# The gathered rows of eight experts: turned into columns by transposing transfers of 16-bit halves instead of by TensorE

## The chip, the core and the metric

The kernel runs on one core of a Trainium2 chip. The metric is the device time of one execution in microseconds (us); three executions of the kernel before took 1567.37, 1568.19 and 1569.07 us, so the median is 1568.19 us. TensorE (PE) does matrix products and transposes, VectorE (DVE) and ScalarE (ACT) work elementwise, GpSimd (POOL) and SyncE (SP) here mostly start transfers (DMAs).

## The reference

A graph layer is followed by a feed-forward stack with a mixture of experts, on 625 tokens of 1024 numbers. Everything is float32.

```
x = x + gnn(layernorm(x), edges)                 # 625 x 1024, 10000 edges
h = layernorm(x) @ lin0_w + lin0_b
h = silu(h @ swi1_w1 + b1) * (h @ swi1_w2 + b2)
scores = softmax(h @ gate_w.T); topv, topi = top_k(scores, 4), renormalised
routed = sum over the 4 chosen experts e: topv_e * ((silu(h @ exp_w1[e]) * (h @ exp_w3[e])) @ exp_w2[e])
shared = (silu(h @ sh_w1) * (h @ sh_w3)) @ sh_w2  # hidden width 2048
h = (routed + shared) @ lin1_w + lin1_b
x = x + silu(h @ swi2_w1 + b1) * (h @ swi2_w2 + b2)
```

## The kernel before

**Arithmetic.** Activations lie with features on the 128 partitions and tokens along the free dimension. A float32 product is made of three faster products: each operand is cut into a high part (a copy in a shorter format) and a low part (the rest), and `hi*hi + hi*lo + lo*hi` is summed in PSUM (`products`, L1793). A weight matrix comes in units of 128 x 1024 numbers (128 output features, 8 input chunks). One unit is one SP transfer of 512 KB into one of four slots of `raw`; ACT writes the high part `w_hi` (L502) and DVE the low part `w_lo` (L1226), also in rings of four; PE then runs 8 chunks x 3 = 24 matmuls. A split waits until PE is done with the unit that was four places earlier, and SP reloads a slot of `raw` when both splits of the unit in it are done (`load_four`, L445).

**The stages.** Graph layer; `lin0` and `swi1`; the first half of the shared expert (`sha`: 16 units up, 8 down, 625 tokens each); the eight experts, fullest first, with 344, 332, 328, 324, 316, 312, 304 and 296 token slots; the second half of the shared expert; `lin1` and `swi2`. While `swi1` runs, its output is also turned to token-major rows (`h_rows`: PE transposes, ACT copies to `rows`, L876 and L878) and written to `h_rows_dram` by one ACT transfer (L907). Routing runs beside the first units of `sha` and leaves for each expert a list of token numbers.

**Into an expert.** POOL gathers the rows of an expert's tokens from `h_rows_dram` into `grow` (a view of `gath`), in three indirect transfers of 128, 128 and 88 rows (`gather`, L573). Features must lie on partitions, so PE transposes each 128-feature chunk `m` in three pieces into a PSUM bank (`expert_in`, L2151); ACT copies that to the high part `e_hi` (L916) and DVE computes the low part `e_lo` (L1569). For the first expert this follows unit `m` of the down projection of `sha`, for the others unit `m` of the down projection of the expert before.

**Through an expert.** Sixteen units up alternate between gate and value: ACT applies silu (L933), DVE multiplies (L1589), ACT and DVE split the product (L936, L1593). Eight units down follow. After each, ACT copies the result out of PSUM (`yt_copied`, L942), and PE turns the copy of the chunk before to rows (`turn_y`, L2172), which DVE copies to `yrow` (L1580, L1581) and POOL stores (L588). In instruction order PE runs down unit `m`, `turn_y(m - 1)`, `expert_in(next, m)`; after `m = 7` comes `turn_y(7)`. ACT runs in group `m`: split of the unit three ahead, copy out (L942), high part of the next expert's chunk (L916). DVE: split of the unit three ahead, `y_rows(m - 1)`, low part of the next expert's chunk.

Of the kernel before, what the change touches and what calls it, by code (L numbers as in the profile page):

```python
# [5 lines left out]
T = 625  # L6
D = 1024
EDGES = 10000
EXPERTS = 8
TOP = 4  # L10
P = 128
KC = D // P
# [12 lines left out]
SLOT_TILES = [(0, P), (P, P), (2 * P, CAP - 2 * P)]  # L25
RING = 4
# [21 lines left out]
def build(nc, x, src, dst, gnn_b, biases, gate, stream, out):  # L48
# [5 lines left out]
    u32 = mybir.dt.uint32  # L54
    ALU = mybir.AluOpType
# [3 lines left out]
    h_rows_dram = nc.dram_tensor("h_rows_dram", (T, D), f32).ap()  # L59
# [5 lines left out]
    with ctx:  # L65
# [16 lines left out]
        silu = sb("silu", [P, TP], f32)  # L82
        prod = sb("prod", [P, 2, TP], f32)
# [37 lines left out]

        acc = ctx.enter_context(nc.psum_tensor("acc", [P, 8, 512], f32))
# [9 lines left out]
        g_hi, g_lo = hl(act_b, KC, CAP)  # L132
# [9 lines left out]
        logits_t = gath[0:GW, D:D + TP]  # L142
        stats = silu[:, 0:NT * 12].rearrange("p (i h s) -> p i h s", i=NT, h=2)
# [209 lines left out]
        xe_tp = sem("xe_tp")  # L353
# [29 lines left out]
        ov_raw = grow[:, 1, :]  # L383
        ov_out = yrow[:, 0, :]
# [46 lines left out]
        def _(sp):  # L431
# [9 lines left out]

            def load_four(done, first):
                for s in range(RING):
                    sp.wait_ge(hi_split, done + (s + 1 - RING))
                    sp.wait_ge(lo_split, done + (s + 1 - RING))  # L445
                    sp.dma_start(raw[:, s, :],
                                 stream[bass.ds(first + s, 1), :, :].rearrange("u p n -> (u p) n")
                                 ).then_inc(raw_loaded[s], 16)
# [22 lines left out]
            with sp.Fori(U_SHA // RING + 1, U_EXP // RING) as g:  # L471
                load_four(g * RING, g * RING)
            sp.wait_ge(order_ready, 1)
            with sp.Fori(0, EXPERTS) as r:
                expert = sp.value_load(order_i[0:1, bass.ds(r, 1)], min_val=0, max_val=EXPERTS - 1)
                with sp.Fori(0, UNITS_EXPERT // RING) as g:
                    load_four(r * UNITS_EXPERT + g * RING + U_EXP, expert * UNITS_EXPERT + g * RING + U_EXP)
# [40 lines left out]
        def _(pool):  # L518
# [48 lines left out]
            def gather(e):  # L567
                pool.tensor_copy(now_tok[:, :], slot_tok[:, bass.ds(3 * e, 3)]).then_inc(now_ready, 1)
                pool.wait_ge(h_saved, 16)
                pool.wait_ge(now_ready, e + 1)  # L570
                pool.sem_inc(gather_go, 1)
                for n, (c0, cn) in enumerate(SLOT_TILES):
                    pool.indirect_dma_start(out=grow[0:cn, n, :], out_offset=None, in_=h_rows_dram,  # L573
                                            in_offset=bass.IndirectOffsetOnAxis(ap=now_tok[0:cn, n:n + 1], axis=0)
                                            ).then_inc(gathered, 16)
# [3 lines left out]
            pool.wait_ge(ln_tp, 2 * NT)  # L579
            gather(0)  # L580
# [10 lines left out]

            pool.wait_ge(xe_tp, KC)
            gather(1)
# [7 lines left out]
            with pool.If(fullest(pool) > CAP):  # L601
                pool.wait_ge(y_saved, 16 * 3 * EXPERTS)
                pool.wait_ge(xe_tp, EXPERTS * KC)
                pool.iota(ov_iota, [[1, OV_ALL]], base=CAP, channel_multiplier=0,
                          allow_small_or_imprecise_dtypes=True).then_inc(ov_ready, 1)
                with pool.Fori(0, OV_ROUNDS) as c:
                    with pool.Fori(0, EXPERTS) as e:
# [3 lines left out]
                        pool.indirect_dma_start(out=ov_in, out_offset=None, in_=h_rows_dram,  # L611
# [20 lines left out]
            pool.wait_ge(xe_tp, EXPERTS * KC)  # L632
# [12 lines left out]
        def _(act):  # L645
# [1720 lines left out]
```

## Time and profile before

| | |
|---|---|
| median of three executions | 1568.19 us |
| profiled execution: its own time | 1567.0 us |
| profiled execution: its span | 1565.3 us |
| share of the span busy: PE, DVE, ACT, POOL | 99%, 55%, 37%, 8% |
| mean traffic of the transfers | 131 GB/s |
| granted clock of TensorE | 0.999 of full speed |

The span runs from the first to the last instruction that the profiler recorded; the execution's own time is 1.7 us more. Matmuls are pipelined: the profile shows one of 312 columns as 309 ns long, although the next one starts about 0.15 us after it. The place of PE in time is therefore read from the chain of waits, which gives each group the time until the next one starts.

### The profile page before, as it was taken

What the parts mean: (1) busy time and instruction counts of PE and PEld (TensorE: products, weight loads), DVE (VectorE), ACT (ScalarE), POOL (GpSimd) and SP (SyncE); (2) the same over time, 40 slices, a digit from 0 to 9 for tenths busy, and PEclk for the clock granted to TensorE, in tenths of its full rate; (3) what the DMA queues carried; (4) which work ended last, traced back from release to release, by engine and by line L of the source; (5) the groups of instructions that cost most, each with busy time, mean ns of one, the idle gap of its engine ahead of it and who ended that gap; (6) DMA issues with size and microseconds to landing.
All of it is one profiled execution on the core that took longest, in us unless ns stands there. A gap on an engine that the chain in (4) does not pass through costs nothing.

```text
span 1565.3 us, 28095 instructions
## 1 busy us (share of the span) xinstructions
PE 1551.4 (99%) x10796; PEld 1534.7 (98%) x10796; DVE 854.2 (55%) x1460; ACT 584.7 (37%) x914; POOL 117.8 (8%) x139
## 2 busy tenths in 40 slices
PE   9999999999999999999999999999999999999998
PEld 9998999999999999999999999999999999999998
DVE  8665569845522344454544545454555366335886
ACT  6332345432222333343444444444444222223442
POOL 1321010000100001000010100001000133001000
PEclk9999999999999999999999999999999999999999
DMA  4412203232422446446464654646555576221333
GB/s 136 133 41 72 76 28 108 82 131 84 123 76 79 157 138 189 151 135 208 137 207 148 191 165 150 202 151 208 161 172 163 160 204 178 83 80 55 94 117 83
DMA packets 71001, 205.64 MB, mean 131 GB/s; under 512 B 13620, under 2 KB 22370, under 8 KB 70890
## 3 DMA queue, kind: packets, MB, share of 16 engines
q1 hardware_dynamic: 45020, 157.94, 32.6%
q0 software_dynamic: 14976, 32.81, 7.0%
q10 hardware_dynamic: 10894, 13.26, 2.7%
q8 instruction: 87, 1.43, 0.4%
q14 instruction: 24, 0.20, 0.0%
HBM read 185.01 MB, written 18.95 MB: 130 GB/s over the span
## 4 chain that ended last, share of the span: by engine, by line
PE 94%; DVE 4%; issue 1%; ACT 1%; ACTq 0%; DVEq 0%; POOL 0%; POOLq 0%
PE acc L1793 86%; PE acc L1773 2%; PE acc L2172 1%; PE acc L2151 1%; DVE w_lo L1277 1%; DVE yrow L1042 0%; PE acc L1842 0%; DVE yrow L1041 0%; ACTq L1000 0%; PE acc L2108 0%; PE acc L1758 0%; PE acc L2225 0%; PE acc L1784 0%; PE acc L1952 0%; DVE acc L1323 0%
## 5 line engine op out<-in xcount | busy, mean ns | idle before, releaser
L1793 PE MATMUL acc<-act_x,w_hi 128*128 128x312 f32 (+8 forms) x2304 | 507.6, 309 | 1.6 <-DVE act_b L1290 0.6
L1793 PE MATMUL acc<-act_b,w_hi 128*128 128x312 f32 (+8 forms) x2048 | 456.0, 311 | 0.0
L1793 PE MATMUL acc<-act_a,w_hi 128*128 128x314 f32 (+1 forms) x1920 | 423.0, 310 | 2.7 <-DVE gath L1349 2.3
L1793 PEld LDWEIGHTS acc<-act_x,w_hi 128*128 128x128 f32 x2304 | 385.3, 188 | 2.5 <-ACT act_a L826 1.0
L1793 PE MATMUL acc<-act_x,w_lo 128*128 128x312 f32 (+8 forms) x1152 | 355.7, 309 | 0.0
L1793 PEld LDWEIGHTS acc<-act_b,w_hi 128*128 128x128 f32 x2048 | 340.2, 189 | 0.1
L1226 DVE TENSOR_TENSOR w_lo<-raw,w_hi 128x1024 fp32r<-128x1024 f32 x253 | 309.0, 1222 | 44.2 <-ACT w_hi L502 43.2
L1793 PEld LDWEIGHTS acc<-act_a,w_hi 128*128 128x128 f32 x1920 | 319.5, 190 | 4.0 <-ACT w_hi L798 2.8
L1793 PE MATMUL acc<-act_b,w_lo 128*128 128x314 f32 (+8 forms) x1024 | 315.6, 308 | 0.0
L1793 PE MATMUL acc<-act_a,w_lo 128*128 128x314 f32 (+1 forms) x960 | 294.9, 307 | 0.0
L502 ACT ACTIVATE w_hi<-raw 128x1024 fp32r<-128x1024 f32 x264 | 277.1, 1051 | 8.3 <-PE acc L1793 4.6
L1793 PEld LDWEIGHTS acc<-act_x,w_lo 128*128 128x128 f32 x1152 | 216.7, 188 | 0.0
L1793 PEld LDWEIGHTS acc<-act_b,w_lo 128*128 128x128 f32 x1024 | 193.0, 188 | 0.0
L1793 PEld LDWEIGHTS acc<-act_a,w_lo 128*128 128x128 f32 x960 | 181.3, 189 | 0.0
L1589 DVE TENSOR_TENSOR prod<-acc,silu 128x344 f32<-128x344 f32 x64 | 33.1, 517 | 249.7 <-PE acc L1793 220.8
L936 ACT ACTIVATE act_b<-prod 128x344 fp32r<-128x344 f32 x64 | 31.5, 493 | 172.1 <-DVE prod L1589 172.1
L942 ACT ACTIVATE prod<-acc 128x344 f32<-128x344 f32 x64 | 29.3, 458 | 133.3 <-PE acc L1793 133.3
L1580 DVE COPY yrow<-acc 128x256 f32<-128x256 f32 x64 | 27.1, 423 | 75.3 <-PE acc L2172 75.3
L933 ACT ACTIVATE silu<-acc 128x344 f32<-128x344 f32 x64 | 29.4, 459 | 102.2 <-PE acc L1793 102.2
L1236 DVE TENSOR_TENSOR prod<-acc,silu 128x628 f32<-128x628 f32 x16 | 13.0, 811 | 99.3 <-PE acc L1793 99.3
L588 POOL DMA_DIRECT2D y_dram<-yrow x24 | 13.5, 563 | 681.1 <-DVE yrow L1581 680.7
L1569 DVE TENSOR_TENSOR act_x<-acc,act_x 128x344 fp32r<-128x344 f32 x64 | 33.1, 517 | 54.5 <-ACT act_x L916 53.9
(239 smaller groups left out, 1247.0 us busy)
## 6 DMA issues: line engine op xcount, KB each, us to landing
raw<-stream_dram SPq DMA_DIRECT2D x296, 512.0 KB, 3.7
y_dram<-yrow POOLq DMA_DIRECT2D x16, 512.0 KB
y_dram<-yrow POOLq DMA_DIRECT2D x8, 352.0 KB
rows<-x_dram ACTq DMA_DIRECT2D x1, 2500.0 KB
x_dram<-rows ACTq DMA_DIRECT2D x5, 500.0 KB
h_rows_dram<-rows ACTq DMA_DIRECT2D x1, 2500.0 KB
rows<-x_dram ACTq DMA_DIRECT2D x8, 312.5 KB
rows<-x_dram SPq DMA_DIRECT2D x5, 448.0 KB
```

The source lines that it names most:

```text
L502: nc.scalar.activation(w_hi[:, s, :], raw[:, s, :], ACT.Copy).then_inc(hi_split, count)
L933: act.activation(silu[:, 0:CAP], acc[:, 2 * m % 4, 0:CAP], ACT.Silu).then_inc(exp.silu, 1)
L936: act.activation(g_hi[:, m, :], prod[:, m % 2, 0:CAP], ACT.Copy).then_inc(exp.hi, 1)
L942: act.activation(prod[:, m % 2, 0:CAP], acc[:, m % 4, 0:CAP], ACT.Copy).then_inc(yt_copied, 1)
L1226: dve.tensor_tensor(w_lo[:, s, :], raw[:, s, :], w_hi[:, s, :].bitcast(f32), ALU.subtract).then_inc(lo_split, count)
L1277: dve.tensor_tensor(wlo8[:, n % 8, :], quad_source(q, t), whi8[:, n % 8, :].bitcast(f32), ALU.subtract).then_inc(dve_quad_lo, 1)
L1569: dve.tensor_tensor(e_lo[:, m, :], acc[:, TPB + 2 + m % 2, 0:CAP], e_hi[:, m, :].bitcast(f32), ALU.subtract).then_inc(xe_lo, 1)
L1580: dve.tensor_copy(yrow[:, 0:2, m * P:(m + 1) * P], b[:, 0:2 * P].rearrange("p (s d) -> p s d", d=P))
L1589: dve.tensor_tensor(prod[:, m % 2, 0:CAP], acc[:, (2 * m + 1) % 4, 0:CAP], silu[:, 0:CAP], ALU.mult).then_inc(exp.prod, 1)
L1773: last = pe.matmul(outs[i], oh_dst[0:TT, s, i * TT:i * TT + rows_of(i)], oh_src[0:TT, s, :], start=False, stop=ends)
L1793: ins = pe.matmul(o, w, xs_[h], start=(first and w is hi and xs_ is x_hi), stop=(last and w is lo))
L2151: last = pe.transpose(acc[:, TPB + 2 + m % 2, c0:c0 + cn], grow[0:cn, n, m * P:(m + 1) * P], ident[0:cn, 0:cn])
```

## The change

The gathered rows go from rows to columns in transfers rather than on PE. Such a transposing transfer handles 16-bit elements, so a float32 row is stored as two planes of 16-bit halves.

- `h_rows`: ACT reads the PSUM bank as 16-bit numbers and writes all first halves of a token's row and then all second halves (`rows16`, `h_rows_dram` of 2048 16-bit numbers per token).
- POOL gathers the same bytes, but for every expert after the first into one staging row per partition, `x_stage`, one third of the list at a time; each next third waits until the staging row has been turned. The first expert's three thirds go to `rows`.
- SP issues `dma_start_transpose` three times for each expert (128, 128 and 96 rows by 2048 halves), into `xe_parts`. For the first expert they follow the loads of the 16 up units of `sha`; for expert `e + 1` they follow the loads of units 11, 15 and 19 of expert `e`. SP's loops over the experts are written out.
- DVE puts the two halves of each number side by side again: one copy of 2 x 344 16-bit numbers for each chunk, into one of two buffers `x32`. ACT and DVE take high and low parts from there and no longer from PSUM.
- `expert_in` leaves PE's program. ACT takes the high part of the next expert's chunk `m` before its copy of unit `m`; DVE makes word `m` and low part `m - 1` before `y_rows(m - 1)`, and low part 7 before `y_rows(7)`.
- `silu` and `prod` become views of one tensor `work`, in which the experts have narrower views beside `x32`. A path for experts with more tokens than slots, which does not run on these inputs, is adapted as well.

```diff
+XR = 352
+YC = 3 * P
+X_TILES = [(0, P), (P, P), (2 * P, XR - 2 * P)]
+X_TURNS = (11, 15, 19)
...
-        silu = sb("silu", [P, TP], f32)
-        prod = sb("prod", [P, 2, TP], f32)
+        work = sb("work", [P, 3 * TP], f32)
...
+        silu = work[:, 0:TP]
+        prod = work[:, TP:3 * TP].rearrange("p (s w) -> p s w", w=TP)
+        e_silu = work[:, 0:CAP]
+        x32 = work[:, CAP:3 * CAP].rearrange("p (s w) -> p s w", w=CAP)
+        e_prod = work[:, 3 * CAP:3 * CAP + 2 * YC].rearrange("p (s w) -> p s w", w=YC)
...
+        x_stage = flat_b[:, 9 * D:10 * D].bitcast(u16)
...
+        xe_parts = gath[:, 0:KC * XR].bitcast(u16).rearrange("p (n s) -> p n s", s=XR)
+        xe_halves = xe_parts.rearrange("p (t k) s -> p t k s", t=2)
+        rows16 = rows[:, :, :].rearrange("p i d -> p (i d)").bitcast(u16).rearrange("p (i t d) -> p i t d", i=NT, t=2)
...
+            def turn_inputs(e, n, source, count):
+                c0, cn = X_TILES[n]
+                sp.wait_ge(gathered, 16 * count)
+                if e >= 1 and n == 0:
+                    sp.wait_ge(x32_ready, e * KC)
+                sp.dma_start_transpose(xe_parts[:, :, c0:c0 + cn], source[0:cn, :]).then_inc(xe_turned, 16)
+
+            with sp.Fori(U_SHA // RING + 1, (U_SHA + UNITS_UP) // RING) as g:
+                load_four(g * RING, g * RING)
+            for n in range(3):
+                turn_inputs(0, n, rows16[:, n, :, :].rearrange("p t d -> p (t d)"), 3)
+            with sp.Fori((U_SHA + UNITS_UP) // RING, U_EXP // RING) as g:
...
+            for r in range(EXPERTS):
+                expert = sp.value_load(order_i[0:1, r:r + 1], min_val=0, max_val=EXPERTS - 1)
+                for j in range(UNITS_EXPERT):
+                    load_one(r * UNITS_EXPERT + U_EXP + j, j % RING, expert * UNITS_EXPERT + U_EXP + j)
+                    if j in X_TURNS and r + 1 < EXPERTS:
+                        n = X_TURNS.index(j)
+                        turn_inputs(r + 1, n, x_stage, 3 * (r + 1) + n + 1)
...
+            def gather_tile(to, n):
+                cn = X_TILES[n][1]
+                pool.indirect_dma_start(out=to[0:cn, :], out_offset=None, in_=h_rows_dram,
+                                        in_offset=bass.IndirectOffsetOnAxis(ap=now_tok[0:cn, n:n + 1], axis=0)
+                                        ).then_inc(gathered, 16)
+
+            def gather_rest(e):
+                for n in range(1, 3):
+                    pool.wait_ge(xe_turned, e * (16 * 3) + 16 * n)
+                    pool.sem_inc(gather_go, 1)
+                    gather_tile(x_stage, n)
...
+            pool.wait_ge(x32_ready, KC)
+            pool.wait_ge(unit_done, U_EXP)
+            gather_list(1)
+            gather_tile(x_stage, 0)
+            gather_rest(1)
             with pool.Fori(1, EXPERTS - 1) as e:
+                pool.wait_ge(x32_ready, e * KC + KC)
+                gather_list(e + 1)
+                gather_tile(x_stage, 0)
                 save_y(e - 1)
-                pool.wait_ge(xe_tp, e * KC + KC)
-                gather(e + 1)
+                gather_rest(e + 1)
...
-                act.activation(rows[0:TT, 0:4, m * P:(m + 1) * P],
-                               acc[0:TT, TPB, :].rearrange("p (i d) -> p i d", d=P), ACT.Copy)
-                act.activation(rows[0:TT, 4, m * P:(m + 1) * P], acc[0:TT, TPB + 1, 0:P],
+                act.activation(rows16[0:TT, 0:4, :, m * P:(m + 1) * P],
+                               acc[0:TT, TPB, :].bitcast(u16).rearrange("p (i d t) -> p i t d", d=P, t=2), ACT.Copy)
+                act.activation(rows16[0:TT, 4, :, m * P:(m + 1) * P],
+                               acc[0:TT, TPB + 1, 0:P].bitcast(u16).rearrange("p (d t) -> p t d", t=2),
                                ACT.Copy).then_inc(h_copied, 1)
...
-                act.wait_ge(xe_tp, e * KC + (m + 1))
-                act.activation(e_hi[:, m, :], acc[:, TPB + 2 + m % 2, 0:CAP], ACT.Copy).then_inc(xe_hi, 1)
+                act.wait_ge(x32_ready, e * KC + (m + 1))
+                act.activation(e_hi[:, m, :], x32[:, m % 2, :], ACT.Copy).then_inc(xe_hi, 1)
...
+                    if nxt:
+                        expert_in_hi(e + 1, m)
                     act.wait_ge(unit_done, base + (UNITS_UP + m + 1))
                     if m >= 2:
                         act.wait_ge(y_tp, e * KC + (m - 1))
-                    act.activation(prod[:, m % 2, 0:CAP], acc[:, m % 4, 0:CAP], ACT.Copy).then_inc(yt_copied, 1)
-                    if nxt:
-                        expert_in_hi(e + 1, m)
+                    act.activation(e_prod[:, m % 2, 0:CAP], acc[:, m % 4, 0:CAP], ACT.Copy).then_inc(yt_copied, 1)
...
+            def expert_in_word(e, m):
+                if m == 0:
+                    dve.wait_ge(xe_turned, e * (16 * 3) + 16 * 3)
+                if m >= 2:
+                    dve.wait_ge(xe_lo, e * KC + (m - 1))
+                dve.tensor_copy(x32[:, m % 2, :].bitcast(u16).rearrange("p (s t) -> p t s", t=2),
+                                xe_halves[:, :, m, 0:CAP]).then_inc(x32_ready, 1)
+
             def expert_in_lo(e, m):
                 dve.wait_ge(xe_hi, e * KC + (m + 1))
-                dve.tensor_tensor(e_lo[:, m, :], acc[:, TPB + 2 + m % 2, 0:CAP], e_hi[:, m, :].bitcast(f32),
+                dve.tensor_tensor(e_lo[:, m, :], x32[:, m % 2, :], e_hi[:, m, :].bitcast(f32),
                                   ALU.subtract).then_inc(xe_lo, 1)
+
+            def expert_in(e, m):
+                expert_in_word(e, m)
+                if m >= 1:
+                    expert_in_lo(e, m - 1)
...
+                    if nxt:
+                        if m == 0:
+                            dve.wait_ge(unit_done, base + UNITS_UP)
+                        expert_in(e + 1, m)
                     if m >= 1:
                         y_rows(e, m - 1)
-                    if nxt:
-                        expert_in_lo(e + 1, m)
+                if nxt:
+                    expert_in_lo(e + 1, KC - 1)
                 y_rows(e, KC - 1)
...
-            def expert_in(e, m):
-                if isinstance(e, int):
-                    if m == 0:
-                        pe.wait_ge(gathered, 16 * 3 * (e + 1))
-                else:
-                    if m == 0:
-                        pe.wait_ge(gathered, e * (16 * 3) + 16 * 3)
-                if m >= 2:
-                    pe.wait_ge(xe_lo, e * KC + (m - 1))
-                for n, (c0, cn) in enumerate(SLOT_TILES):
-                    last = pe.transpose(acc[:, TPB + 2 + m % 2, c0:c0 + cn], grow[0:cn, n, m * P:(m + 1) * P],
-                                        ident[0:cn, 0:cn])
-                last.then_inc(xe_tp, 1)
...
+                    if e == 0 and j in (0, 2):
+                        pe.wait_ge(sha_y, KC - 1 + j // 2)
...
                         turn_y(e, m - 1)
-                    if nxt:
-                        expert_in(e + 1, m)
...
-            pe.wait_ge(sha_y, KC)
```

## Rows read from the trace of the kernel before

**Rows 1.** The page: span, busy time by engine, chain that ended last.

```profile
span 1565.3 us, 28095 instructions
PE 1551.4 (99%) x10796; PEld 1534.7 (98%) x10796; DVE 854.2 (55%) x1460; ACT 584.7 (37%) x914; POOL 117.8 (8%) x139
PE 94%; DVE 4%; issue 1%; ACT 1%; ACTq 0%; DVEq 0%; POOL 0%; POOLq 0%
```

**Rows 2.** Chain of waits in order of time: start us, us until the next, what.

```profile
509.97 0.70 ACT rows L923
...
575.64 3.82 PE acc L1793 x24
...
606.09 0.33 PE acc L2172 x3
606.42 0.30 PE acc L2151 x3
606.72 0.47 PE acc L2172 x3
...
1121.17 3.38 PE acc L1793 x24
1124.55 0.33 PE acc L2172 x3
```

**Rows 3.** Line L2151 alone: op, count, ns min/median/max, first and last start, forms.

```profile
L2151 PE MATMUL acc<-ident,gath x192: 240/272/273, 458.7 to 1144.9; 128*128 128x128 f32 x128, 88*128 88x88 f32 x64
```

**Rows 4.** Timeline of ACT: start us, us, line, op, out<-in, [idle before].

```profile
606.13 0.46 ACT L942 ACTIVATE prod<-acc 128x344 f32<-128x344 f32 x1 [2.41 <-PE acc L1793]
...
666.32 0.49 ACT L936 ACTIVATE act_b<-prod 128x344 fp32r<-128x344 f32 x1 [2.89 <-DVE prod L1589]
666.72 1.05 ACT L502 ACTIVATE w_hi<-raw 128x1024 fp32r<-128x1024 f32 x1
669.33 0.46 ACT L942 ACTIVATE prod<-acc 128x344 f32<-128x344 f32 x1 [1.57 <-PE acc L1793]
```

**Rows 5.** Timeline of DVE, same columns.

```profile
667.80 1.23 DVE L1226 TENSOR_TENSOR w_lo<-raw,w_hi 128x1024 fp32r<-128x1024 f32 x1
```

**Rows 6.** Groups of instructions by form on DVE: count, busy us, mean ns.

```profile
L1226 DVE TENSOR_TENSOR w_lo<-raw,w_hi 128x1024 fp32r<-128x1024 f32 x253 | 309.0, 1222 | 44.2 <-ACT w_hi L502 43.2
L1569 DVE TENSOR_TENSOR act_x<-acc,act_x 128x344 fp32r<-128x344 f32 x64 | 33.1, 517 | 54.5 <-ACT act_x L916 53.9
L1617 DVE TENSOR_SCALAR yrow<-gath,top_w 125x1024 f32<-125x1024 f32 x5 | 3.7, 745 | 0.0
```

**Rows 7.** Transfers by issue: count, size, us from issue to landing.

```profile
raw<-stream_dram SPq DMA_DIRECT2D x296, 512.0 KB, 3.7
gnn_bias<-gnn_b_dram SPq DMA_DIRECT2D x1, 4.0 KB, 10.9
```

**Rows 8.** Timeline of DVE in the seventh expert.

```profile
1066.99 1.22 DVE L1226 TENSOR_TENSOR w_lo<-raw,w_hi 128x1024 fp32r<-128x1024 f32 x1
...
1075.30 1.23 DVE L1226 TENSOR_TENSOR w_lo<-raw,w_hi 128x1024 fp32r<-128x1024 f32 x1
1080.01 0.52 DVE L1589 TENSOR_TENSOR prod<-acc,silu 128x344 f32<-128x344 f32 x1 [3.48 <-PE acc L1793]
1080.44 1.22 DVE L1226 TENSOR_TENSOR w_lo<-raw,w_hi 128x1024 fp32r<-128x1024 f32 x1
```

**Rows 9.** Timeline of ACT in the seventh expert.

```profile
1076.55 0.46 ACT L933 ACTIVATE silu<-acc 128x344 f32<-128x344 f32 x1 [1.28 <-PE acc L1793]
1078.41 1.06 ACT L502 ACTIVATE w_hi<-raw 128x1024 fp32r<-128x1024 f32 x1 [1.40 <-DMA raw<-stream_dram]
```

**Rows 10.** Timeline of ACT around `h_rows`, near the end of `swi1`.

```profile
315.14 0.58 ACT L876 ACTIVATE rows<-acc 125x512 f32<-125x512 f32 x1
...
316.63 0.94 ACT L831 ACTIVATE gath<-acc,bias 128x314 f32<-128x314 f32 x2 [0.74 <-DVE acc L1398]
```

**Rows 11.** Busy time by stretch, fourth to sixth expert: window, us; PE, PEld, DVE, ACT, POOL; clock, DMA share, GB/s.

```profile
791.70:1059.20 267.50, 267.50 (x1873) 266.93 (x1873) 134.30 (x193) 113.28 (x168) 14.53 (x21) 1.00 0.55 173
```

More of the change, by code:

```diff
@@ L131, in build @@
         e_hi, e_lo = hl(act_x, KC, CAP)
-        g_hi, g_lo = hl(act_b, KC, CAP)
+        flat_b = act_b[:, :, :].rearrange("p s n -> p (s n)")
+        g_hi, g_lo = [flat_b[:, s * KC * CAP:(s + 1) * KC * CAP].rearrange("p (k w) -> p k w", w=CAP)
+                      for s in range(2)]
+        x_stage = flat_b[:, 9 * D:10 * D].bitcast(u16)
         h_hi, h_lo = hl(act_b, NT, D)
@@ L383, in build @@
         ov_raw = grow[:, 1, :]
+        ov_x = grow[:, 2, :]
+        ov_words = sem("ov_words")
         ov_out = yrow[:, 0, :]
@@ L440, in _, with load_one @@
             sp.dma_start(bias[:, :, :], biases).then_inc(small_loaded, 16)
+            def load_one(done, s, u):
+                sp.wait_ge(hi_split, done + (1 - RING))
+                sp.wait_ge(lo_split, done + (1 - RING))
+                sp.dma_start(raw[:, s, :], stream[bass.ds(u, 1), :, :].rearrange("u p n -> (u p) n")
+                             ).then_inc(raw_loaded[s], 16)
             def load_four(done, first):
                 for s in range(RING):
[L444 to L448, printed above, removed]
+                    load_one(done + s, s, first + s)
             def load_seven(L):
@@ L571, in gather @@
                 pool.sem_inc(gather_go, 1)
-                for n, (c0, cn) in enumerate(SLOT_TILES):
-                    pool.indirect_dma_start(out=grow[0:cn, n, :], out_offset=None, in_=h_rows_dram,
-                                            in_offset=bass.IndirectOffsetOnAxis(ap=now_tok[0:cn, n:n + 1], axis=0)
-                                            ).then_inc(gathered, 16)
+            def gather_tile(to, n):
[8 more added lines that the diff above has]
+                    gather_tile(x_stage, n)
             pool.wait_ge(routed, 1)
             pool.wait_ge(tok_copied, 1)
-            pool.wait_ge(ln_tp, 2 * NT)
-            gather(0)
+            gather_list(0)
+            for n in range(3):
+                gather_tile(rows16[:, n, :, :].rearrange("p t d -> p (t d)"), n)
             pool.wait_ge(tok_copied, 4)
@@ L610, in _ @@
                         pool.sem_inc(ov_go, 1)
-                        pool.indirect_dma_start(out=ov_in, out_offset=None, in_=h_rows_dram,
+                        pool.indirect_dma_start(out=ov_in.bitcast(u16), out_offset=None, in_=h_rows_dram,
                                                 in_offset=bass.IndirectOffsetOnAxis(ap=now_tok[:, 0:1], axis=0)
@@ L906, in _ @@
             act.wait_ge(h_copied, KC)
-            act.dma_start(h_rows_dram.rearrange("(i p) d -> p i d", p=TT), rows[0:TT, :, :]).then_inc(h_saved, 16)
+            act.dma_start(h_rows_dram.rearrange("(i p) d -> p i d", p=TT),
+                          rows16[0:TT, :, :, :].rearrange("p i t d -> p i (t d)")).then_inc(h_saved, 16)
             for m in range(KC):
@@ L1588, in expert @@
                     dve.wait_ge(exp.silu, e * KC + (m + 1))
-                    dve.tensor_tensor(prod[:, m % 2, 0:CAP], acc[:, (2 * m + 1) % 4, 0:CAP], silu[:, 0:CAP],
+                    dve.tensor_tensor(e_prod[:, m % 2, 0:CAP], acc[:, (2 * m + 1) % 4, 0:CAP], e_silu,
                                       ALU.mult).then_inc(exp.prod, 1)
@@ L2162, in _ @@
                 dense(U_SHA + UNITS_UP, m, b_hi, b_lo, both(sha.hi, sha.lo) if m == 0 else None)
-                if m == 0:
-                    pe.wait_ge(tok_copied, 4)
-                expert_in(0, m)
             def turn_y(e, m):
@@ L2171, in turn_y @@
                 for n, (c0, cn) in enumerate(SLOT_TILES):
-                    last = pe.transpose(acc[0:cn, TPB + m % 2, n * P:(n + 1) * P], prod[:, m % 2, c0:c0 + cn],
+                    last = pe.transpose(acc[0:cn, TPB + m % 2, n * P:(n + 1) * P], e_prod[:, m % 2, c0:c0 + cn],
                                         ident[:, :])
```

38 lines of the change are left out of this document (18 added, 20 removed).

## The prediction

> **What bounds the kernel now.** The page comes first: PE is busy 99% of the span and holds 94% of the chain that ended last [rows 1]. So the time is the sum of what PE is given, and something that leaves PE's program shortens it unless PE has to wait at that place for something else. The second view is the chain of waits, read over the experts for what lies between two weight units. The reader sees a steady beat: 24 matmuls (3.82 us in the widest expert, 3.38 us in the seventh), `turn_y` 0.33 us, `expert_in` 0.30 us [rows 2]. Third come the timelines of ACT and DVE. These engines don't bound anything there now, yet the change gives DVE a copy and changes the order on both, so it matters how far they are from the beat. Last come the transfers, since transposing ones are put into the queue that also loads the weights.
>
> **What goes from PE.** `expert_in` is 192 transposes, which is 8 experts x 8 chunks x 3 pieces [rows 3]. The profiler gives one 272 ns, but they are pipelined and the chain gives a group of three 0.30 us [rows 2], which is the price I use. Now place by place:
> - Chunks 0 to 6 for the seven later experts: 7 x 7 x 0.30 = 14.7 us. PE has the next unit's weights ready there, so all of it counts.
> - Chunk 7 of those seven: nothing. Today unit 7 ends at 606.09, and `turn_y(6)` and `expert_in` fill the time to 606.72. But `turn_y(7)` needs ACT's copy of unit 7, which starts at 606.13 and takes 0.46 us [rows 2, 4]. With `expert_in` gone PE reaches that wait 0.30 us earlier and stands there for about as long.
> - The first expert's chunks, beside the down units of `sha`: 7 x 0.30 = 2.1 us. After the eighth unit PE now waits for ACT's copy out, 0.70 us, with its own `expert_in` under that wait [rows 2]. The change lets the first two expert units start before this copy, since they write banks that the seventh unit used. So 0.7 us more goes.
> Sum: 14.7 + 2.1 + 0.7 = 17.5 us.
>
> **What DVE and ACT get.** DVE's new copy has 688 16-bit numbers per partition. The trace has no such copy. With two SBUF-side inputs or PSUM, DVE does about one number per cycle: 344 numbers take 517 ns and 1024 take 1222 ns, so 1.04 ns each and 160 ns fixed [rows 6]. By that the copy takes 688 x 1.04 + 160 = 0.88 us. But an operation with one tensor input, SBUF to SBUF, did 1024 numbers in 745 ns [rows 6], which is 0.57 ns each beyond the fixed part, and so 0.55 us for 688. I take 0.55, because this copy is of the same kind (one input, both sides in SBUF). The writing with gaps of one number may spoil it, so I keep 0.88 as the ordinary other end, and twice the slow slope, 1.6 us, as the far one; nothing can make it cheaper than zero, which would change nothing in the sum.
> The Trainium skill, VectorE: DVE Perf Modes, "What auto-detection actually checks", says the same of that kind: two numbers per cycle when the single source and the destination are in SBUF and the outermost counts are even, with no condition on the step. The 745 ns agree with it for step 1; step 2 in the output is not in this trace. By that rule the sum stays 17.5 less the 0.3 below; without it, it is the second rival's.
>
> Why the copy matters although DVE is busy 50% there (134.3 of 267.5 us) [rows 11]: it closes a loop between two engines. ACT's copy of unit `m` now stands behind the high part of chunk `m`, which waits for DVE's word `m`, which stands behind the weights' low part, which waits for ACT's split, which follows ACT's copy of unit `m - 1`. Start to start: copy out 0.36, split to low part 1.08, low part 1.13, word, high part 0.40 and about 0.04 for the hand-over [rows 4, 5] (the copy's 0.46 and the low part's 1.23 overlap what follows by 0.1). That is 3.01 us plus the word: 3.56 with 0.55. The beat of PE after the change is unit plus `turn_y`: 3.82 + 0.33 = 4.15 us in the widest expert and 3.38 + 0.33 = 3.71 in the seventh [rows 2]. A loop shorter than the beat loses nothing in the long run. It starts late, though: in group 0, split (666.72) and low part (from 667.80) come as now, the word ends about 669.5, and the copy out starts at 669.9 instead of 669.33 [rows 4, 5], 0.6 us late, up to 0.9 in narrow experts. Group 1 has no `turn_y` in its beat and adds up to 0.2; the other six give back 0.15 each or more. At `turn_y(7)`, the one place where PE feels it, 0.3 us is left in the seventh expert and none elsewhere. I subtract 0.3: 17.2 us.
>
> **What hides the rest.** `h_rows` on ACT copies twice as many, half as long, numbers: at most twice 0.58 for the large piece [rows 10]. That hides in the idle time before L831 (0.74 us), where ACT waits for DVE anyway; with that cover gone it would be 8 x 0.8 = 6 us. High and low parts read SBUF instead of PSUM: the same sizes from SBUF took 0.49 (L936) against 0.46 us (L942) [rows 4], inside the loop's slack. POOL gathers as many bytes as before and has nothing urgent behind it. DVE's low part 7 moves between `y_rows(6)` and `y_rows(7)`, some 1.6 us after the last unit, while PE wants it at the eighth chunk of the next unit, over 3 us after; free.
>
> **The transposing transfers.** 21 of them, 512 KB or less each, go into SP's queue (and three for the first expert, some 50 us early). Call T the time from SP's issue until the queue is free for the next load. Behind load 11, 15 or 19 stands the even load 12, 16 or 20, and these are the steps until PE feels it, in the seventh expert. The slot of the even unit is released 5.1 us after the odd one's (low parts end at 1076.53 and 1081.66) [rows 8]. The load is wanted 8.7 us after its issue (slot free at 1068.21, split due at 1076.90 behind silu) [rows 8, 9] and takes 3.7 alone [rows 7], so 5.0 more. The low part waits for DVE's product until 1080.44, so 1.0 more [rows 8, 9]. PE takes up that unit eight units after 1059.7, at 1086.6, and the low part ends at 1081.66: 4.9 more. In all T may be 16.0 us. The trace supports this: the load for the split at 1078.41 took 10.2 us, and PE did not stop. T itself: the nearest row is the same amount through the same queue, 3.7 us; the far one is a transfer of 4 KB in 4-byte pieces, 10.9 us [rows 7], by which 2-byte pieces would take milliseconds. I take the near one, doubled since both ends are SBUF: about 7 us, hidden. Traffic allows it: the transfer engines are 55% busy there [rows 11], and 3 x 7 us in a 90 us expert adds at most 23 points.
> The Trainium skill has two figures for T that disagree. DMA: Bandwidth & Descriptors, "Latency and other measured facts", gives a transposing transfer 261 GB/s, an estimated 2 us for 512 KB. VectorE: DVE Perf Modes, "The three transpose paths", gives 1309 ns for one 128 x 128 piece of 16-bit numbers, an estimated 21 us for sixteen pieces in a row, which would be the first rival. No row here decides between them.
>
> **Sum.** The profiled execution took 1567.0 us (span 1565.3, 1.7 around it), 1.2 below the median of 1568.2. 1568.2 - 17.2 = 1551.0 us.
>
> **Rivals.**
> 1. *The transposing transfers hold up the weights: slower.* Each microsecond of T beyond 16.0 stops PE 21 times. The gain of 17.2 is gone at T = 16.8; at T = 18 the time is 1551 + 42 = 1593, at 20.4 (twice the crowded load) 1551 + 92 = 1643. If SP itself is held while it issues, it is the same sum. For it: nothing in the trace shows such a transfer being cheap, and each is followed at once by loads. Against it: 16 us is over four times a plain transfer, and each one has four units, about 14 us, to itself. Chance 0.22, of which 0.03 within 0.2% of before and the rest slower.
> 2. *The copy runs at one number per cycle.* The loop takes 3.89 us. The lag at `turn_y(7)` is 0 in the widest expert and grows to 0.9 + 0.3 + 0.5 + 6 x 0.18 = 2.8 us in the seventh (late start, the slower first word, group 1 without `turn_y`, six beats that are too short); about 1.3 on average, 9 us in seven experts. Gain 8.5, time 1559.7. At 1.6 us for the copy the lags reach 5 to 8 us and the sum is a loss; I fold that into the slower chance. Chance 0.15, of which 0.02 slower and 0.02 the same.
> 3. *The transfers only fray the beat:* gathers, stores and turns meet, some splits come late, and half of the gain is lost: 1560. For it: the wait of 1.40 us for a load that is already there [rows 9]. Chance 0.09.
>
> **How the numbers follow.** Forecast 0.54, with its own range 1548.5 (the eighth groups also gain, 7 x 0.30 = 2.1) to 1556. Two in ten may be left out; these are the far part of the first rival, so the range goes from 1548 up to 1593. A measurement of this kernel tells 0.2%, 3.1 us, from no change. Faster: 0.54 + 0.11 + 0.09 = 0.74; same: 0.03 + 0.02 = 0.05; slower: 0.19 + 0.02 = 0.21.
>
> **What would show it.** Right: the chain has no L2151 and no new waiter in the experts, and beats are 4.15 to 3.71 us; `turn_y(7)` follows ACT's copy; the new DVE copy takes near 0.55 us; the transposing transfers end within 7 us or so, and ACT's waits for `raw` are no longer than now. Rival 1: ACT's L502 waits for `raw` after units 12, 16 and 20, and PE's first long idle times lie in the up phase. Rival 2: the copy is near 0.88 us, and PE idles 1 to 3 us at `turn_y(7)` for ACT's copy, most in the narrow experts. Most of all, T above 16 us would make the prediction wrong.

## The result

The changed kernel takes 1550.2 us (median of 4 runs, 1549.98 to 1550.35), the kernel before 1568.6 (1567.4 to 1569.5): a ratio of 0.9885, with an interval of 0.9873 to 0.9896. The prediction was 1551.0. The medians are 18.4 us apart, the profiled executions (1567.0 and 1550.2) 16.8 us; 17.2 were forecast.

The page of the changed kernel (span, busy time by engine, chain that ended last), against [rows 1]:

```profile
span 1548.6 us, 27511 instructions
PE 1531.0 (99%) x10604; PEld 1513.5 (98%) x10604; DVE 874.5 (56%) x1524; ACT 587.7 (38%) x914; POOL 117.4 (8%) x139
PE 92%; DVE 4%; ACT 2%; issue 1%; DMA 1%; SPq 0%; ACTq 0%; DVEq 0%
```

PE has 192 matmuls less and is still busy 99% of the time, so the end came forward with its work. In the chain of waits (start us, us, what), against [rows 2], `expert_in` is missing, `turn_y` is L2226, and at chunk 7 the chain goes over ACT's copy L994:

```profile
597.26 3.80 PE acc L1864 x24
...
601.08 0.47 ACT work L994
...
601.60 0.55 PE acc L2226 x3
602.14 65.77 PE acc L1864 x432
...
1104.10 3.33 PE acc L1864 x24
1107.43 0.33 PE acc L2226 x3
```

The timeline of DVE in the seventh expert has the new copy, L1622. That of ACT shows its loop with the high part (L966) ahead of the copy of the unit (L994):

```profile
1103.93 0.56 DVE L1622 COPY work<-gath 128x688 uint16<-128x688 uint16 x1
```

```profile
1101.37 0.44 ACT L994 ACTIVATE work<-acc 128x344 f32<-128x344 f32 x1
...
1104.53 0.49 ACT L966 ACTIVATE act_x<-work 128x344 fp32r<-128x344 f32 x1 [1.77 <-DVE work L1622]
1104.92 0.44 ACT L994 ACTIVATE work<-acc 128x344 f32<-128x344 f32 x1
```

The copy takes 0.56 us (forecast 0.55), the loop 1104.92 - 1101.37 = 3.55 (forecast 3.56), and a beat of PE in that expert 3.33 + 0.33 = 3.66.

Transfers by issue (count, KB each, us from issue to landing), against [rows 7], and a later stretch of the same kind as [rows 11], same columns:

```profile
raw<-stream_dram SPq DMA_DIRECT2D x296, 512.0 KB, 3.7
...
gath<-act_b SPq DMA_TRANSPOSE x21, 6.7
```

```profile
782.46:1043.21 260.75, 260.10 (x1803) 259.23 (x1802) 142.06 (x217) 112.55 (x169) 14.37 (x22) 1.00 0.69 195
```

A transposing transfer lands 6.7 us after its issue (forecast about 7), and the share of the transfer engines rose by 14 points, from 0.55 to 0.69. Weights came no later: 3.7 us as before.

**Where the time went.** Three marks in both traces:

- Up to the logits' matmuls: 343.58 us before, 344.30 after.
- From there to the first unit of the first expert: 167.13 and 163.77, so 3.4 us less (2.8 forecast for the `sha` stage).
- From there to the first matmul behind the last expert: 723.67 and 709.48, so 14.2 less. Up to the first unit of the eighth expert it is 635.46 and 619.72, so 15.7 less, which the groups explain. The eighth expert itself takes 88.21 and 89.76, so 1.5 more: there PE has a new gap, which the profile shows as 1.27 us (below).

The rest is equal to 0.1 us: 0.7 - 3.4 - 14.2 + 0.1 = -16.8. The first mark is not steady. The last matmul stage ahead of the experts starts at 438.56, 438.03 and 439.95 us in traces whose program is the same up to there. So single totals differ by a microsecond or two without a cause in the experts, and I compare stretches wherever I can.

### The profile page after: what moved, and what is told of

The parts are those of the page before. It is cut to its first block, busy times and chain, and to the rows that moved or that the text cites. A ratio compares the mean times of both kernels' runs of the same rounds, so it can differ in the third digit from the quotient of the medians.

```text
span 1548.6 us, 27511 instructions
## 1 busy us (share of the span) xinstructions
PE 1531.0 (99%) x10604; PEld 1513.5 (98%) x10604; DVE 874.5 (56%) x1524; ACT 587.7 (38%) x914; POOL 117.4 (8%) x139
## 4 chain that ended last, share of the span: by engine, by line
PE 92%; DVE 4%; ACT 2%; issue 1%; DMA 1%; SPq 0%; ACTq 0%; DVEq 0%
PE acc L1864 86%; PE acc L1844 2%; PE acc L2226 1%; DMA rows<-x_dram 1%; DVE w_lo L1327 1%; PE acc L1913 0%; DVE yrow L1091 0%; ACT act_b L701 0%; DVE yrow L1092 0%; PE acc L2179 0%; PE acc L2278 0%; PE acc L1855 0%; PE acc L2023 0%; ACT act_b L706 0%; ACT work L994 0%
## 5 line engine op out<-in xcount | busy, mean ns | idle before, releaser
L1653 DVE TENSOR_TENSOR work<-acc,work 128x344 f32<-128x344 f32 x64 | 33.1, 517 | 251.5 <-PE acc L1864 251.5
L986 ACT ACTIVATE act_b<-work 128x344 fp32r<-128x344 f32 x64 | 31.5, 492 | 174.9 <-DVE work L1653 174.9
L966 ACT ACTIVATE act_x<-work 128x344 fp32r<-128x344 f32 x64 | 31.4, 491 | 100.2 <-DVE work L1622 100.2
L983 ACT ACTIVATE work<-acc 128x344 f32<-128x344 f32 x64 | 29.3, 458 | 105.6 <-PE acc L1864 105.6
L1286 DVE TENSOR_TENSOR work<-acc,work 128x628 f32<-128x628 f32 x16 | 13.0, 811 | 95.5 <-PE acc L1864 95.5
L1844 PE MATMUL acc<-yrow 125*125 125x314 bf16 (+1 forms) x400 | 55.6, 297 | 2.5 <-DVE yrow L1092 2.5
L1844 PEld LDWEIGHTS acc<-yrow 125*125 125x125 bf16 (+1 forms) x400 | 52.9, 136 | 4.1 <-DVE yrow L1092 4.1
L834 ACT ACTIVATE act_b<-work 128x628 fp32r<-128x628 f32 x16 | 11.7, 731 | 98.8 <-DVE work L1286 98.8
```

The source lines that it names most:

```text
L834: act.activation(o_hi[:, m, :], prod[:, m % 2, :], ACT.Copy).then_inc(st.hi, 1)
L966: act.activation(e_hi[:, m, :], x32[:, m % 2, :], ACT.Copy).then_inc(xe_hi, 1)
L983: act.activation(e_silu, acc[:, 2 * m % 4, 0:CAP], ACT.Silu).then_inc(exp.silu, 1)
L986: act.activation(g_hi[:, m, :], e_prod[:, m % 2, 0:CAP], ACT.Copy).then_inc(exp.hi, 1)
L1286: dve.tensor_tensor(halves(prod[:, m % 2, :]), acc_dense(1), halves(silu[:, :]), ALU.mult).then_inc(st.prod, 1)
L1653: dve.tensor_tensor(e_prod[:, m % 2, 0:CAP], acc[:, (2 * m + 1) % 4, 0:CAP], e_silu, ALU.mult).then_inc(exp.prod, 1)
```

## Experiments

Ratios and times are against runs of the kernel before on the same chip (medians 1567.5 to 1568.0). The changed kernel was run again on the chip of experiment 7 and of the second run of experiment 8; it took 1550.0 (1549.8 to 1552.3, ratio 0.9888 [0.9873, 0.9903]).

> The changed kernel itself, beside the others on the same chip: 1550 us. It is to tell whether last_turn_later's 3 us hold on one chip.

**1. TensorE's groups put back, chunks 0 to 6.** The results are not used.

```diff
                     if m >= 1:
                         turn_y(e, m - 1)
+                    if nxt and m in range(7):
+                        for n, (c0, cn) in enumerate(SLOT_TILES):
+                            pe.transpose(acc[:, TPB + 2 + m % 2, c0:c0 + cn], ident[0:cn, :], ident[0:cn, 0:cn])
```

> The changed kernel with three TensorE transposes of a constant put back behind turn_y of chunks 0 to 6 in seven experts, 49 groups in all; their result is used by nothing. My theory: in the weight stream TensorE waits for nothing at these places, so each group costs what the chain showed, 0.30 us (0.335 by how much the groups before and after the change differ): 14.7 to 16.4 us more, 1564.9 to 1566.6 us. The rival, that the gain came from the transfers and the engines' order and not from TensorE's program: less than 5 us more, under 1555 us.

Measured: 1565.9 us (1564.1 to 1567.5), ratio 0.9985 [0.9976, 0.9994]: 15.7 more. The chain of this kernel (L2260 is the group put back):

```profile
576.98 0.33 PE acc L2226 x3
577.30 0.29 PE acc L2260 x3
577.60 3.81 PE acc L1864 x24
```

From the last stage ahead of the experts (438.62) to the eighth expert (1143.78) it takes 705.16 us, the changed kernel (438.56 to 1127.79) 689.23. That is 15.93 / 49 = 0.325 a group: 0.30 for itself, and the unit behind it is 3.82 in place of 3.79. (In the seventh expert the group also hides 0.4 us of PE's wait at `turn_y(7)`, so the price of one is nearer to 0.33.) PE's program is the gain; the rival falls.

**2. The same for chunk 7 alone** (`m in (7,)`).

> The same three TensorE transposes put back behind turn_y of chunk 7 alone, seven groups. My step says that chunk 7 gains nothing. They stand behind turn_y(7) here, where the next expert's first unit starts, so in the kernel before they stood ahead of turn_y(7), under the wait for ScalarE's copy; put behind it, they are no longer covered. My theory: 7 x 0.30 to 0.335 = 2.1 to 2.3 us more, 1552.4 us. The rival, that something else (a bank or the first weights of the next expert) is late at this place and hides them: 1550.2 us.

Measured: 1549.5 us (1548.6 to 1550.5), ratio 0.9879 [0.9864, 0.9895]. Nothing is lost, and my expectation was wrong: it put the group behind `turn_y(7)`. The program order is unit 7, `turn_y(6)`, the group, `turn_y(7)`, the very place that `expert_in` had. The chain:

```profile
602.62 0.33 PE acc L2226 x3
602.95 0.30 PE acc L2260 x3
603.24 0.47 PE acc L2226 x3
603.71 65.77 PE acc L1864 x432
```

From the end of unit 7 to the next expert's first unit it is 603.71 - 602.62 = 1.09 us; without the group, 602.14 - 601.06 = 1.08. Over all seven experts, from the last stage ahead of them (439.95) to the eighth (1129.41), it is 689.46 against 689.23 in the changed kernel: 0.2 us for seven groups, where the expectation had 2.1 to 2.3. PE's waits at `turn_y` sum to 0.3 us against 1.9. So the step of the prediction (chunk 7 gains nothing) is shown. I had only placed my own experiment wrongly.

**3. A second copy on VectorE ahead of each word.**

```diff
+                if not isinstance(e, int) or e >= 1:
+                    dve.tensor_copy(gath[:, KC * XR:KC * XR + 324].bitcast(u16).rearrange("p (s t) -> p t s", t=2),
+                                    xe_halves[:, :, m, 0:324])
                 dve.tensor_copy(x32[:, m % 2, :].bitcast(u16).rearrange("p (s t) -> p t s", t=2),
```

> The changed kernel with a second copy of 648 16-bit numbers on VectorE ahead of each chunk's own copy, from the second expert on (into columns that nothing reads). About 0.53 us more per chunk. My theory of the loop between the two engines: it grows from 3.55 to about 4.05 us, while the beats of TensorE are 4.1 us in the widest expert down to 3.67 in the seventh, so ScalarE's copy of a unit falls behind from chunk to chunk and TensorE waits at turn_y(7), between 0.7 us more in the second expert and 3 us more in the eighth: 13 to 15 us in all, 1563 to 1565 us. The rival, that VectorE is half idle and hides it: 1550 to 1551 us.

Measured: 1569.3 us (1565.7 to 1570.3), ratio 1.0004 [0.9995, 1.0013]: a copy of 0.53 us takes back the whole gain. The chain in the seventh expert runs through both engines:

```profile
1116.38 0.53 DVE gath L1623
1116.91 0.45 DVE work L1625
...
1117.79 0.44 ACT work L994
...
1121.75 0.44 ACT work L994
```

The loop is 1121.75 - 1117.79 = 3.96 us (forecast 4.05), longer than the beats of the narrow experts. PE's waits by cause (us in total, times, longest), first of this kernel, then of the changed one:

```profile
PE acc L2229 <- ACT work L994: 15.7, 7, 3.4
```

```profile
PE acc L2226 <- ACT work L994: 1.9, 7, 0.6
```

That is 13.8 us more, as the theory has it. The other 2 us of this trace (5 of the medians) go with a lower clock, which I had not counted: 0.995 to 0.998 over the runs of this kernel, 0.999 to 1.000 over those of the changed one. After the wait of 3.4 us in the seventh expert, a stretch of PE (window, length, PE busy, clock, DMA share, GB/s) shows:

```profile
1143.00:1146.00 3.00, 2.83 (x13) 0.61 0.33 131
```

A granted clock of 0.61 is a stretch largely at the lower level, 1.2 GHz.

**4. The same, with ScalarE's order as before.** The two lines of `expert_in_hi(e + 1, m)` stand behind the copy of unit `m`.

> The second copy on VectorE as in word_twice, but ScalarE copies out unit m before it makes the high part of chunk m, as in the kernel before. My theory: the high part (0.40 us) and the wait for the word no longer stand in the loop, which then is copy out, split, low part: well under the beats. So the second copy costs nothing: 1550 to 1551 us. The rival, that word_twice costs what it does because VectorE has too much to do: the same time as word_twice.

Measured: 1551.1 us (1549.2 to 1551.9), ratio 0.9891 [0.9874, 0.9907]. The same work on VectorE now costs nothing that can be told from zero. It was the order that closed the loop, and not VectorE's load.

**5. The wait ahead of the first expert put back.**

```diff
-                    if e == 0 and j in (0, 2):
-                        pe.wait_ge(sha_y, KC - 1 + j // 2)
...
+            pe.wait_ge(sha_y, KC)
             for e in range(EXPERTS - 1):
```

> The changed kernel with TensorE's wait for ScalarE's copy out of the eighth down unit of sha put back where it was, before the first expert's first unit. My step priced it at 0.7 us: 1550.9 us. If the wait has become shorter, since turn and copy stand otherwise now: 1550.2 us.

Measured: 1551.9 us (1549.7 to 1553.0), ratio 0.9902 [0.9885, 0.9918]. The medians are too coarse for 0.7 us; the timeline has it, where the changed kernel's PE has no idle time:

```profile
507.81 0.58 PE L1864 MATMUL acc<-act_x,w_hi 128*128 128x344 f32 x2 [0.78 <-ACT rows L973]
```

**6. The transposing transfers made longer.** Each of the 21 is issued twice (three times, with `range(2)`), and SP waits until one has landed before it issues the next. The edit for twice:

```diff
+                for again in range(1):
+                    if e >= 1:
+                        n_again = ((e - 1) * 3 + n) * 1 + again + 1
+                        sp.dma_start_transpose(xe_parts[:, :, c0:c0 + cn], source[0:cn, :]).then_inc(turned_again, 16)
+                        sp.wait_ge(turned_again, 16 * n_again)
                 sp.dma_start_transpose(xe_parts[:, :, c0:c0 + cn], source[0:cn, :]).then_inc(xe_turned, 16)
```

> The changed kernel with each transposing transfer of the seven later experts' rows issued twice, one after the other through the same queue, SyncE waiting for the first before it goes on. The time T from issue until the next load may be issued grows by the time of one such transfer, about 6 to 7 us, to 12 to 14 us. My theory, a tolerance of 16 us: TensorE does not feel it, 1550 to 1552 us. The first rival in its general form (any microsecond for which SyncE is held reaches TensorE): 21 x 6.5 = 136 us more, 1687 us.

> The same with each transposing transfer issued three times: T of about 19 to 21 us, beyond the tolerance of 16 us. My theory: 21 x 3 to 5 = 63 to 105 us more, 1613 to 1655 us, with TensorE waiting at the unit after next of each even load. If the tolerance is far larger than I worked out: 1550 us; if it is smaller: above 1660 us.

Measured: 1568.3 us (1563.2 to 1575.1), ratio 1.0006 [0.9989, 1.0023], and 1658.8 (1657.5 to 1659.4), ratio 1.0580 [1.0562, 1.0598]. Twice, at T = 11 us, was to cost nothing and cost 18 us; the tolerance of 16 us is wrong. The chain of the doubled kernel in the seventh expert:

```profile
1069.78 6.74 DMA gath<-act_b
1076.54 4.26 DMA gath<-act_b
...
1081.59 8.59 DMA act_b<-h_rows_dram,now_tok
1090.19 4.24 DMA gath<-act_b
1094.45 4.26 DMA gath<-act_b
...
1099.51 7.64 DMA act_b<-h_rows_dram,now_tok
1107.17 3.81 DMA gath<-act_b
1110.99 3.71 DMA gath<-act_b
1114.73 0.56 DVE work L1628
```

The three pieces share one staging buffer. So the gather of the second piece starts only when the first has been turned, and turn, gather, turn, gather, turn is one chain. It ends at the next expert's first word (L1628), a deadline of which the prediction says nothing. The changed kernel has the same chain with room. Its third piece is issued at 1087.60 and lands 6.5 us later, at 1094.1, and the word starts at 1100.38 (SP's timeline; the transfer view of the third piece's window, with us to landing; the word):

```profile
1087.60 1.79 SPq L496 DMA_TRANSPOSE gath<-act_b  x1
```

```profile
gath<-act_b SPq DMA_TRANSPOSE x1, 6.5
```

```profile
1100.38 0.56 DVE L1622 COPY work<-gath 128x688 uint16<-128x688 uint16 x1
```

That is 6.3 us of room for three turns in one chain: T can grow by 2.1 us each, to an estimated 8.8. SP issues the second and the third piece 0.6 us after their gathers have landed, which adds 0.4 us at most. At the other six boundaries the room is 5.5 to 8.6 us. In the doubled kernel the word comes 1114.73 - 1069.78 = 44.95 us after the first piece's issue, in the changed one, whose first piece is issued at 1060.71, 39.67: 5.3 late. The repeats add 4.26 + 4.26 + 3.71 = 12.2, less the 6.3 makes 5.9. That this comes out so near is partly luck: the pieces themselves land 6.6 us sooner in sum than in the changed kernel, and the steps from a landing to the next piece take 5.9 us more. VectorE stands idle before the first word at five of the seven boundaries, for 1.9 to 5.2 us; at the first two the word is in time.

Issued three times, the cost is 108.6 / 7 = 15.5 us a boundary, just above my range of 63 to 105 us in all. PE's waits in that trace:

```profile
PE acc L2232 <- ACT work L1000: 52.3, 14, 7.8
PE acc L1870 <- ACT work L989: 22.4, 6, 5.4
PE acc L1870 <- DVE act_b L1663: 5.4, 1, 5.4
```

The first row is the late word, some 7 us a boundary. The other two are seven waits, one a boundary, and come from late weights: ACT's splits just ahead of them waited 9.7 to 12.5 us for their load. So both limits are passed here. Together the waits are 78.2 us longer than in the changed kernel, the span is 108.8 longer, and the other 31 go mostly with the clock, 0.975 on average.

**7. Two checks of that deadline.** Doubled, but two units sooner; and once, but four units later:

```diff
-X_TURNS = (11, 15, 19)
+X_TURNS = (9, 13, 17)
```

```diff
-X_TURNS = (11, 15, 19)
+X_TURNS = (15, 19, 23)
```

> turned_x2 (each transposing transfer twice) with the three pieces sent behind the loads of units 9, 13 and 17 in place of 11, 15 and 19, two units or about 7 us sooner. New theory: turned_x2 lost its time because the third piece lands 4.7 us after VectorE wants the next expert's first word (a deadline that my prediction did not look at), not because weights were late. Two units sooner the piece is there in time: 1550 to 1553 us. The rival, my first reading (SyncE held longer than the tolerance for the weights): as turned_x2, 1564 to 1569 us.

> The changed kernel, each transposing transfer once, with the three pieces sent behind the loads of units 15, 19 and 23, four units or 13.4 to 14.6 us later. The first word is wanted 8.5 us after the third piece lands in the seventh expert and 9.6 us after in the second, so the word comes about 5 us late in each of seven experts, as in the seventh expert of turned_x2, where TensorE waited 3.4 us and its clock fell. New theory: 7 x 3.4 to 3.8 us and up to 2.3 us each for the clock: 1574 to 1592 us. The rival (only what holds up the weights counts; each hold is as short as now): 1550 us.

Later: 1598.8 us (1596.3 to 1601.2), ratio 1.0196 [1.0183, 1.0210]. The rival, by which only held weights count, falls: here nothing is held longer. In that trace (timeline of PE in the seventh expert; then PE's waits):

```profile
1148.14 0.90 PE L2226 MATMUL acc<-ident,work 128*128 128x128 f32 x3 [5.21 <-ACT work L994]
```

```profile
PE acc L2226 <- ACT work L994: 33.5, 14, 5.2
```

The span is 46.4 us longer: 31.6 more waiting, where 24 to 27 were expected, since I had reckoned the room as 8.5 us by the shortest turn (4.3 us to landing) and not by this one's 6.5; and 14.8, or 2.1 a boundary, mostly for the clock. The next unit takes 5.23 us in place of 3.34.

Sooner: 1566.3 us (1561.9 to 1568.3), ratio 0.9990 [0.9981, 0.9999], and not 1550 to 1553. The traced execution is the fastest of the eleven. PE's waits, first doubled, then doubled and sooner:

```profile
PE acc L2232 <- ACT work L1000: 13.2, 14, 3.4
```

```profile
PE acc L1870 <- DVE act_b L1663: 8.5, 2, 4.4
...
PE acc L2232 <- ACT work L1000: 1.5, 7, 0.2
```

The late words are gone as the theory says, but late weights have taken their place. The row names DVE, and its cause is the load, as ACT's timeline tells:

```profile
1106.53 1.06 ACT L542 ACTIVATE w_hi<-raw 128x1024 fp32r<-128x1024 f32 x1 [7.27 <-DMA raw<-stream_dram]
```

SP had stood from 1088.0 until 1096.13 for the gather and until 1101.9 for the turns, 13.9 us in all. So the prediction's first rival is real as well, and it begins below a hold of 16 us. The wait for the gather adds to T. And PE waits here not for the late unit itself, which is the third down unit, but for the last chunk of the product in the first: ACT takes the high part of that chunk only behind the split that waits for the load. The 16 us follow a late load to its own unit and leave this way out; they were also worked out for other units than those of this placement. In the seventh expert a T of 11 us breaks the one limit or the other, and moving the pieces only trades them.

**8. The last wait in the experts taken away.**

```diff
                     unit(base, j, e_hi, e_lo, (j % 4,), WIDTHS[e], in_ready if j == 0 else None)
+                    if j == 0 and e >= 1:
+                        turn_y(e - 1, KC - 1)
...
                     dense(U_SHB, 0, a_hi, a_lo)
-                turn_y(e, KC - 1)
+                    turn_y(e, KC - 1)
```

> The changed kernel with turn_y(7) of seven experts moved behind the first unit of the next expert. My theory: TensorE's wait for ScalarE's copy at turn_y(7), 0.47 to 0.61 us at each of seven places, goes, and nothing is late behind it, since y_rows(7) has the whole first unit of the next expert to spare: 3.3 to 4.3 us less, about 1546.5 us. The rival, that the first unit of the next expert then waits itself (its word or its weights are not there yet): 1550 us, the wait stands one place further on.

> last_turn_later, and ScalarE copies out unit m before it makes the high part of chunk m, as in the kernel before. In last_turn_later nothing in the experts waits for ScalarE's copy any more, so by my theory the second edit has nothing to take away: the same as last_turn_later, 1547 us. The rival, that the order also delays turns or splits that the waits do not show: 1545 us or less.

Measured: 1547.2 us (1545.9 to 1548.5), ratio 0.9867 [0.9852, 0.9882]; with the order 1547.4 (1546.6 to 1549.3), ratio 0.9870 [0.9855, 0.9886]. The second ran on the same chip as the repeat of the changed kernel (1550.0), the first on another. The intervals overlap a little, but the spans of the traces say the same: 1545.4 and 1545.0 against 1548.6 and 1548.2 us. No wait at `turn_y` is left:

```profile
602.37 3.65 PE acc L1864 x24
606.02 0.33 PE acc L2226 x3
```

So about 3 us more are to be had. The order on ScalarE adds nothing to it, but by experiment 4 it would be the safer one.

## Why the prediction was right, and where it was not

- **Chunks 0 to 6, 14.7 us:** right, a little low. The traces give 15.7, putting them back 15.9. A group costs 0.32 to 0.33 us, because the unit behind it is also 0.03 longer.
- **Chunk 7, nothing:** right, shown by experiment 2.
- **The `sha` stage, 2.1 + 0.7 us:** right. The stage is 3.4 shorter, and the wait alone is 0.78.
- **The new copy and the loop:** 0.56 for 0.55 and 3.55 for 3.56 us. The Trainium skill's rule for VectorE (VectorE: DVE Perf Modes, "What auto-detection actually checks") holds here with a step of 2 in the output too. In the seventh expert PE waits 0.61 us at `turn_y(7)` against 0.22 in the wide ones, so the lag is 0.39 for 0.3. That the loop was near its limit, the second rival's reason, is shown by experiments 3 and 4. The rival itself falls by the 0.56.
- **T, about 7 us:** right in size, 6.7. Repeated at once, with no load ahead of it, a turn of 512 KB mostly takes 4.25 us. Of the two estimates by the Trainium skill, 2 us (DMA: Bandwidth & Descriptors, "Latency and other measured facts") is too low, and 21 us (VectorE: DVE Perf Modes, "The three transpose paths") far too high.
- **T may be 16.0 us:** wrong. The step counted how long the weights behind a turn may wait, and took for granted that the gathered rows lie ready and that nobody waits for the third piece. The runs showed an earlier limit in the seventh expert, an estimated 8.8 us (9.2 with the slack before the issues), which is 2.1 above the T of this kernel and not 9.3. At T = 11 the time is 18 us longer (experiment 6), and the first rival gave that case no cost. The limit for the weights is wrong too: a hold of 13.9 us already stopped PE for 4.4 (experiment 7), by way of ACT's order. In the kernel with three issues the late weights stopped PE once a boundary, where the rival counted three. The time came out right all the same because T was 6.7 us. The forecast of 7 was a plain transfer's row doubled by an argument, so that it fell inside a margin of 2 us in place of 9 is in part luck.
- **The third rival, a frayed beat:** no row of it. Weights land in 3.7 us as before, and SP never waits for a gather of the seven experts.
- **`h_rows` on ACT:** hidden, as far as the first mark can tell (0.7 us later, and unsteady by more than that); not tested by itself. The large piece takes 1.02 us (at most 1.16 forecast).

What the sum left out: a gap of 1.27 us in which PE waits for nothing that the profile shows, behind `turn_y(6)` of the last expert.

```profile
1217.55 0.53 PE L1864 MATMUL acc<-act_a,w_hi 128*128 128x314 f32 x2 [1.27 <-issue]
```

A gap of 0.8 to 1.5 us is there in every trace of the changed kernel and its variants but those of experiments 1 and 2, and the kernel before hasn't it either: it is missing where PE has groups of three more in the experts. In the second run of the changed kernel it stands under another name:

```profile
1217.24 0.53 PE L1864 MATMUL acc<-act_a,w_hi 128*128 128x314 f32 x2 [1.47 <-ACT w_hi L536]
```

That name is a coincidence. ACT's split of that time starts 0.79 us after PE's `turn_y(6)` in the changed kernel (1216.57 and 1215.78), and as much after it in experiment 2 (1218.19 and 1217.40), where PE goes on at once:

```profile
1217.65 0.54 PE L1864 MATMUL acc<-act_a,w_hi 128*128 128x314 f32 x2
```

So PE can go on there without that split. The gap comes and goes with instructions far from it, and the transfers hint at why. Queue 8 carries transfers of the kind `instruction`, 16 KB each, 87 in the kernel before and 86 in the changed one. One of them ends at 1215.92, 1.63 us before PE goes on (queue, kind: count, MB, share, window 1214.5 to 1216):

```profile
q8 instruction: 1, 0.02, 5.2%
```

In all eleven traces with the gap PE goes on 1.61 to 1.63 us after the end of such a transfer, although the gap itself is 0.8 to 1.5 us long. In the three without it none ends there: the nearest is within 0.3 us of PE's next unit, the one before it over 4 us earlier. So PE probably waits there for its own next instructions, and fewer of them ahead of this place shift where a block ends. No experiment tried that, so it is not shown. Without the gap the gain would be some 1.5 us larger (the eighth expert takes 89.76 us with the gap, and 88.21 before and 88.24 in experiment 2 without it), and since it is missing in experiments 1 and 2, their totals stand about that much too low; the stretches compared there end before it.

## What to carry to other kernels

Take work from the bounding engine where it waits for nothing; a group that stood under a wait is worth nothing until the wait itself is moved. Before another engine takes the work over, add up the loop between the helpers start to start and compare it with the beat: here 0.5 us more on an engine that is half idle cost 19 us, and an exchange of two instructions made it free. For a transfer, ask for every deadline behind it: who waits for its data, what is queued behind it, and which transfer can start only when its buffer is free.

## What was not expected of the hardware

- A long wait can cost more than its length. After waits of 2.7 to 5.2 us TensorE ran at a granted clock of 0.50 to 0.61, and in the seventh expert the next unit took 5.2 to 5.7 us in place of 3.34; in the doubled kernel (same columns as above):

```profile
1116.00:1120.00 4.00, 3.79 (x16) 0.50 1.02 402
```

  0.50 is the lower of the two levels, 1.2 GHz. Behind waits of 0.5 and 0.6 us (changed kernel, 1127 to 1130) it is 1.00. It does not fall each time: in experiment 3 it did after a wait of 2.7 us (964 to 968: 0.57) and not after one of 3.1 (1052 to 1060: 1.00).
- A turn behind weight loads in the queue took 6.5 to 8.1 us to land in the seventh expert of the changed kernel, and the repeats in the doubled one 3.7 to 4.3. So much of T may be the queue's; that was not tried by itself.
